# A pre-norm transformer block on one core: one key projection of 512 columns per group, and the combine weights' transposes behind the shared expert's gate and up

## The reference

```python
x = x + attn(layernorm(x), Wq, Wk, Wv, Wo)          # 16 heads of 8, local windows of 64 keys
...
scores = einsum('bhnqd,bhnkd->bhnqk', qb, k2) * scale   # mask: j > i and j <= i + 64
p = softmax(where(mask, scores, -1e30)); out = p @ v2
...
x = x + ffn(layernorm(x))
...
topk_idx, topk_weight = gate(x)                     # 16 experts in 4 groups, 2 groups and 4 experts kept
g = einsum('nh,ehm->enm', x, w_gate); u = einsum('nh,ehm->enm', x, w_up)
y = sum over experts of combine * ((silu(g) * u) @ w_down)
shared = (silu(x @ sw_gate) * (x @ sw_up)) @ sw_down
```

## Time and profile before

| | |
|---|---|
| median of 3 runs | 814.77 us (814.01 to 815.94) |
| the profiled execution | 814.36 us, of which the span from first to last instruction is 812.6 us |
| TensorE busy | 740.3 us (91%), 5984 matmuls |
| TensorE weight loads | 611.7 us (75%) |
| GpSimd / ScalarE / VectorE busy | 618.8 us (76%) / 607.7 us (75%) / 525.1 us (65%) |
| mean granted TensorE clock | 0.977 of full speed |

### The profile page before, as it was taken

One profiled execution on the slowest core, in us unless ns is written; L12 is line 12 of the kernel. 1 busy time (PEld: TensorE's weight loads), 2 busy tenths in 40 slices (PEclk: granted clock), 3 DMA queues, 4 the chain that ended last, 5 costly groups with the idle time before them and its releaser, 6 DMA issues.

```text
span 812.6 us, 19809 instructions
## 1 busy us (share of the span) xinstructions
PE 740.3 (91%) x5984; PEld 611.7 (75%) x5984; DVE 525.1 (65%) x1735; ACT 607.7 (75%) x1816; POOL 618.8 (76%) x842
## 2 busy tenths in 40 slices
PE   2568889999999999999999999999999999998876
PEld 1446668787887878787887878787887878786755
DVE  3456686767767676767667676767767575764332
ACT  4787788788787888878788788878787888863332
POOL 3525467879888888978888888988888887956876
PEclk9698899999999999999999999999999999999999
DMA  5000022040413213040312213040313203041321
GB/s 155 26 1 15 14 74 73 15 136 10 120 40 97 63 53 105 2 133 22 105 52 92 65 42 115 2 129 26 105 52 90 67 31 114 3 122 37 117 92 41
DMA packets 50738, 53.86 MB, mean 66 GB/s; under 512 B 5632, under 2 KB 31744, under 8 KB 50560
## 3 DMA queue, kind: packets, MB, share of 16 engines
q1 hardware_dynamic: 50688, 53.25, 21.5%
HBM read 44.31 MB, written 4.72 MB: 60 GB/s over the span
## 4 chain that ended last, share of the span: by engine, by line
PE 45%; POOL 26%; issue 16%; ACT 8%; DMA 2%; DVE 2%; POOLq 1%; SPq 0%; ACTq 0%; DVEq 0%
POOL gate L470 9%; PE PS L1053 8%; PE PS L979 7%; PE PS L869 7%; PE PS L911 6%; PE PS L870 5%; PE PS L871 5%; ACT probs L602 4%; POOL hh L473 4%; POOL q_lo L452 4%; POOL k_lo L462 2%; PE PS L972 2%; PE PS L1050 2%; POOL X L432 1%; PE PS L1014 1%
## 5 line engine op out<-in xcount | busy, mean ns | idle before, releaser
L602 ACT ACTIVATE probs<-PS,neg_max 128x96 f32<-128x96 f32 (+1 forms) x1024 | 245.8, 353 | 60.1 <-DVE neg_max L798 59.4
L470 POOL TENSOR_TENSOR gate<-gate,spread 128x512 f32<-128x512 f32 x128 | 164.2, 1283 | 64.4 <-DMA spread<-weights_by_expert 47.2
L750 DVE STREAM_TRANSPOSE probsT<-probs 128x384 f32<-128x384 f32 (+1 forms) x256 | 124.0, 522 | 101.8 <-ACT probs L602 101.8
L473 POOL TENSOR_TENSOR hh<-gate,tu 128x512 f32<-128x512 f32 x128 | 164.5, 1285 | 17.2 <-POOL gate L470 11.9
L786 DVE SCALAR_TENSOR_TENSOR tu<-th,PS 128x512 f32<-128x512 f32 x128 | 87.9, 687 | 89.3 <-PE PS L871 56.4
L1053 PE MATMUL PS<-wd,hh 128*128 128x128 f32 x1024 | 136.1, 276 | 9.6 <-POOL hh L473 9.6
L1053 PEld LDWEIGHTS PS<-wd,hh 128*128 128x128 f32 x1024 | 126.6, 192 | 15.1 <-POOL hh L473 9.4
L798 DVE TENSOR_REDUCE neg_max<-PS 128x4 f32<-128x384 f32 (+1 forms) x256 | 125.4, 513 | 8.2 <-PE PS L979 5.4
L869 PE MATMUL PS<-x_hi,w_hi 128*128 128x512 f32 x288 | 125.0, 434 | 1.0 <-DVE hs L834 1.0
L560 ACT ACTIVATE th<-PS 128x512 f32<-128x512 f32 x128 | 79.7, 623 | 59.6 <-PE PS L871 59.2
L871 PE MATMUL PS<-x_lo,w_hi 128*128 128x512 f32 x288 | 114.5, 397 | 0.0
(11 more groups left out here) (108 smaller groups left out, 1362.1 us busy)
## 6 DMA issues: line engine op xcount, KB each, us to landing
spread<-weights_by_expert SPq DMA_DIRECT2D x256, 128.0 KB, 3.0
X<-x SPq DMA_DIRECT2D x32, 256.0 KB, 3.4
OUT<-H SPq DMA_DIRECT2D x16, 256.0 KB, 3.0
out<-OUT SPq DMA_DIRECT2D x16, 256.0 KB, 3.1
probsT<-w_gu SPq DMA_DIRECT2D x1, 1152.0 KB, 8.0
wd<-w_down SPq DMA_DIRECT2D x1, 512.0 KB, 9.0
weights_by_expert<-cT SPq DMA_DIRECT2D x16, 32.0 KB, 1.6
probsT<-w_att SPq DMA_DIRECT2D x1, 264.0 KB, 3.5
```

Of the source, the lines that this page charges most:

```text
L470: tt(gate2[:, :], gate[:, k % 2, :], spread[:, k % SP_BUFS, :], ALU.mult).then_inc(s_g2, 1)
L473: tt(hh[:, k % 2, :], gate2[:, :], tu[:, k % 2, :], ALU.mult).then_inc(s_h, 1)
L602: ins = nc.scalar.activation(probs[:, u % 2, tt, a, j0:KW], PS[:, tt, a * KW + j0:a * KW + KW], ACT.Exp, bias=neg_max[:, tt, a:a + 1])
L750: ins = v_.transpose(probsT[:, b, :, t0 + tt, c0:3, :].rearrange("p g c q -> p g (c q)"), probs[:, u % 2, tt, :, c0 * Q:KW])
```

## The change

Two edits. First, the keys of both sequences are projected together: one use `KP = 6` in place of `(6, 8)`, so three matmuls of 512 columns in step 6 and none in step 0. `kr_hi` and `kr_lo` become 512 wide, and the later copies read their half. The shared banks get 14 uses per slot, before 15. Second, in step 3 TensorE runs `gate_up` of the shared expert before the transposes of `comb`, and ScalarE takes its tanh before it copies `cT`. VectorE's order in step 3 stays as it was.

```diff
-KP = (6, 8)
+KP = 6
...
-    (EARLY, (VP, KP[0], LG)), (LATE, (XT, QP, KP[1], XT2, XT2 + 4)),
+    (EARLY, (VP, KP, LG)), (LATE, (XT, QP, XT2, XT2 + 4)),
...
-        kr_hi = sb("kr_hi", [P, T], F32R)
-        kr_lo = sb("kr_lo", [P, T], F32R)
+        kr_hi = sb("kr_hi", [P, TOK], F32R)
+        kr_lo = sb("kr_lo", [P, TOK], F32R)
...
-                                tt(k_lo[:, a, T * b:T * b + T], kr_lo[:, :].bitcast(F32),
+                                tt(k_lo[:, a, T * b:T * b + T], kr_lo[:, T * b:T * b + T].bitcast(F32),
...
-                    def keys(b):
-                        g, _ = at(sl, s, KP[b])
-                        if g:
-                            side, bank = filled(act, sl, s, KEY_PLACE[b])
-                            if not (g.fixed and g.n == 0 and b == 0):
-                                act.wait_ge(s_k_hi, g.n * GB + b)
-                            copy(kr_hi[:, :], bank[:, 0:T]).then_inc(s_high[side], 1)
-
-                    keys(0)
+                    g, _ = at(sl, s, KP)
+                    if g:
+                        side, bank = filled(act, sl, s, EARLY)
+                        if not (g.fixed and g.n == 0):
+                            act.wait_ge(s_k_hi, g.n * GB)
+                        copy(kr_hi[:, :], bank).then_inc(s_high[side], 1)
...
+                    g, _ = at(sl, s, SH)
+                    if g:
+                        act.wait_ge(s_g, g.n * NF + 1)
+                        if not (g.fixed and g.n == 0):
+                            act.wait_ge(s_fa, g.n)
+                        nc.scalar.activation(th[:, :], PS[:, 4, :], ACT.Tanh, scale=0.5).then_inc(s_th, 1)
                     g, _ = at(sl, s, CT)
                     if g:
                         side, bank = filled(act, sl, s, WEIGHTS)
...
-                    keys(1)
...
-                    def keys(b):
-                        g, _ = at(sl, s, KP[b])
-                        if g:
-                            side, bank = free(KEY_PLACE[b])
-                            r = slice(T * b, T * b + T)
-                            exact3(bank[:, 0:T], *w2(WK), xT_hi[:, r], xT_lo[:, r]).then_inc(s_filled[side], 1)
-
-                    keys(0)
+                    g, _ = at(sl, s, KP)
+                    if g:
+                        side, bank = free(EARLY)
+                        exact3(bank, *w2(WK), xT_hi[:, :], xT_lo[:, :]).then_inc(s_filled[side], 1)
...
+                    g, _ = at(sl, s, SH)
+                    if g:
+                        gate_up(g, NP, 0)
+
                     g, _ = at(sl, s, CT)
...
-                    g, _ = at(sl, s, SH)
-                    if g:
-                        gate_up(g, NP, 0)
-
-                    keys(1)
```

More of the change, by code:

```diff
@@ L68 @@
 EARLY, POST, WEIGHTS, LATE = range(4)
-KEY_PLACE = (EARLY, LATE)
 USES = sorted([(stage % STEPS, place, stage) for place, stages in (
-    (EARLY, (VP, KP[0], LG)), (LATE, (XT, QP, KP[1], XT2, XT2 + 4)),
+    (EARLY, (VP, KP, LG)), (LATE, (XT, QP, XT2, XT2 + 4)),
     (POST, (OT, OT + 4, ON, ON + 4, OW, OW + 4)), (WEIGHTS, (CT,)))
@@ L74 @@
 assert len({use[:2] for use in USES}) == len(USES)
-SPLIT = (*zip(KEY_PLACE, KP), (LATE, XT), (LATE, QP), (LATE, XT2), (LATE, XT2 + 4))
+SPLIT = ((EARLY, KP), (LATE, XT), (LATE, QP), (LATE, XT2), (LATE, XT2 + 4))
 LOOP_FIRST, LOOP_END = 6, NG
@@ L456, in slot @@
                         if g:
-                            taken(pool, sl, KP[b] % STEPS, KEY_PLACE[b])
+                            if b == 0:
+                                taken(pool, sl, KP, EARLY)
                             if not (g.fixed and g.n == 0):
@@ L627, in slot @@
                         if g:
-                            taken(act, sl, KP[b] % STEPS, KEY_PLACE[b])
+                            if b == 0:
+                                taken(act, sl, KP, EARLY)
                             if not (g.fixed and g.n == 0):
@@ L632, in slot @@
                             for a in range(HG):
-                                ins = copy(k_hi[:, a, T * b:T * b + T], kr_hi[:, :].bitcast(F32),
+                                ins = copy(k_hi[:, a, T * b:T * b + T], kr_hi[:, T * b:T * b + T].bitcast(F32),
                                            scale=headrow[:, a:a + 1])
@@ L775, in slot @@
                                          ALU.add).then_inc(s_y, 1)
-                    keys(0)
+                    g, _ = at(sl, s, KP)
+                    if g:
+                        side, bank = high_out(sl, s, EARLY)
+                        if not (g.fixed and g.n == 0):
+                            dve.wait_ge(s_k_lo, HG * g.n * GB)
+                        split_low(kr_lo[:, :], bank, kr_hi[:, :]).then_inc(s_taken[side], 1)
                     g, _ = at(sl, s, LN1)
```

## The result

The changed kernel takes 846.47 us (median of 4 runs, 843.95 to 847.97) against 814.44 us (814.01 to 815.94): ratio 1.0387, 95% interval 1.0357 to 1.0416. It is 32 us slower, and I had forecast 8.3. The profiled execution took 843.95 us (span 841.8), 2.5 under the median.

A forecast was written before the change was run, and what follows sets the result against it. TensorE was taken as the bound, busy 44.97 of 46.0 us per slot. Terms 4.4 + 2.3 - 0.3 + 0.9 + 1.0 = 8.3 us on 814.36 gave 822.7, stated as 823, range 819 to 828.

The forecast's parts named there:

- No new wait comes of it: Shared banks, used 14 times per slot in place of 15: every fill waits as before, so no wait is added.
- Leg 1: From TensorE's XT2 transposes over ScalarE, VectorE and 18 us of GpSimd to `comb`: 23.1 us, whatever TensorE does.
- leg 2: From `comb` to the next slot's XT2 transposes, about 22.9 us on TensorE alone; added work lengthens the slot in full.
- the wait ahead of `ve`: GpSimd's idle time before L431, where leg 1 starts: to grow by about 0.5 us from 3.04 us.
- The keys: Wider projection in step 6 adds 0.34 us per slot, 4.4 us over 13; removing step 0's 0.44 us gives nothing back.
- The wait for `up_taken`: Before gate and up in step 3, ended by `tu`: 0.18 us per slot, 2.3 us in all; slot 3 gives back 0.3.
- The last slots: Later transposes and spread tiles: +0.9 us in slot 17 (between 0.4 and 1.9) and +1.0 us in slot 18.
- The clock: TensorE's granted clock in full slots stays 1.00 despite about 1.6 us idle, as after the wait at 784 to 787.
- The keys cost nothing: Rival, chance 0.12: leg 1 starts at an earlier result than TensorE's L1032, so 0.34 us is absorbed: 817.0 us.
- faster: Rival, chance 0.13: the wait for `comb` goes and `tu` comes in time, in each full slot: 801.8 us.
- no change: Rival, chance 0.07: `tu` 0.5 us earlier cancels the keys, or the tail hides its delay: 813 to 816 us.
- The clock's 841: Rival, chance 0.06: the clock falls in each slot, gate and up run at half speed, 18 us more: 841 us.

The follow-up runs named there:

- ten memsets: The changed kernel with ten 128x1 memsets more on VectorE in slot 0, ahead of its loop: 827.66 us, 1.0166 of the kernel before.
- 562: VectorE's loop start in the kernel before (814.44 us), and in the changed kernel with ten memsets in slot 0 (827.66 us).
- 692: The changed kernel with 140 memsets on VectorE ahead of its loop, which then starts at instruction 692: 827.30 us.
- 722: The changed kernel with 170 memsets on VectorE in slots 1 to 5, so that its loop starts at instruction 722: 834.04 us.
- 552: The changed kernel without padding, VectorE's loop starting at instruction 552: 846.47 us, 1.0387 of the kernel before.
- 808: The kernel before, without either edit, with 246 memsets on VectorE in slots 1 to 5, loop start 808: 831.85 us, 1.0219.
- the nine matmuls: Second edit alone, plus nine extra 128x128 matmuls on TensorE ahead of its waits for `hh` in slots 17 and 18: 822.70 us.
- the old order: Second edit alone, but slots 17 and 18 run transposes before gate and up: 818.98 us; on the whole change with ten memsets: 822.87 us.

## Why the prediction was wrong

**The step that failed** is one that isn't there: the sum counts every instruction by the engine's time for it, and none by its place in the engine's program. "No new wait comes of it" was said of semaphores, and holds for them; the new wait is for instructions. It costs 18.8 us of the 32.0 (the changed kernel with and without ten memsets), and 16 can be read off the trace: from `comb` to `comb` on GpSimd the four slots that hold a stall last 50.5 to 50.9 us, those beside them mostly 46.7.

What the runs show of it: with a body of 355 or 358 instructions, starts of 562 and 692 have no stall, 722 one of 2.6 us of idle time per turn, 552 and 808 one of 5.3 to 5.9. All five fit if VectorE holds two blocks of 256 instructions and one block ends 0 to 9 instructions behind 553, so that others end at 809 to 818 and at 1065 to 1074. At 562 and 692 the body lies within two blocks (from 692 on it ends at 1047). At 722 it ends at 1077, in a third, and the jump back finds its target gone. At 552 and 808 it spans three as well, and its first block is left within a few instructions, so that VectorE would stand still for the second block too. The Trainium skill has this rule in Runtime: NRT & Kernel Launch, section Instruction fetch mechanics: blocks of 256 instructions, two of them in most engines, and a taken branch whose target is not in the two has to wait for a fetch. The traces agree, and add the size. That it is the second block that doubles the stall at 552 is argued from the lengths 2.6 and 5.5, with as many packets at both; the blocks themselves were not seen, and their size is the page's. That the place of the loop makes the stall is shown: ten memsets take it away, and padding brings it into a kernel without either edit.

**Leg 1, leg 2** were right: the table above has +0.34 us in B for the keys, and taking away the start of leg 1 took the wait for `comb` away, with 0.8 us per slot. One sign that I had named failed: the wait ahead of `ve` was to grow by 0.5 us, and in the normal slots it is 3.12 us against 3.04.

**The keys**, 4.4: measured 5.6 with the loop in its old place. The mechanism was right; A also grows by 0.04 us (25.00 against 24.96 on the mean of two slots), 4.8 to 4.9 over 13 slots. The rest is in the tail, at which I took nothing: in the traces slot 17 is 0.8 us longer. That taking the second projection out gives nothing back is right too, but not where the time goes: 0.36 us, of which the wait for `comb` takes 0.09. And TensorE's own work falls by 0.02 to 0.03 us per slot, not 0.10.

**The wait for `up_taken`**, 2.3 - 0.3: measured 4.2. The wait stood where I put it, ended by `tu`, and the hand-over of 0.05 us held in every second slot; in the others it was 0.13. Mis-sized was what follows: the same four transposes take 0.43 us ahead of L1032 and took 0.35 ahead of gate and up, and gate and up 1.50 in place of 1.47. I had carried times from one order over to another. That is 0.28 us per slot, 0.36 in every second, and not 0.18.

**The last slots**, 0.9 + 1.0: measured 4.1 and, on the whole change, 4.8. Slot 18 is +1.0 as forecast. In slot 17 I named both ends, 0.4 and 1.9, and each came in some traces. With the second edit alone, with the nine matmuls and with ten memsets most of gate and up ran at the lower level (`cT` 1.8 to 2.0 us later behind `comb` than with the old order). In the profiled run of the changed kernel itself they ran at full speed, 1.50 us, and `cT` came 1.92 us behind the start of `comb`, before 1.49:

```profile
769.37 0.50 PE L862 MATMUL PS<-x_hi,w_hi 128*128 128x512 f32 x1 [0.99 <-DVE tu L780]
...
770.87 0.60 PE L1007 MATMUL PS<-cst,comb 128*16 128x128 f32 x4
...
780.31 1.13 PE L1041 MATMUL PS<-wd,hh 128*128 128x128 f32 x8 [3.45 <-POOL hh L473]
...
812.98 2.05 PE L1041 MATMUL PS<-wd,hh 128*128 128x128 f32 x8 [3.59 <-POOL hh L473]
```

And I had no term for what the later spread tiles do to TensorE: its wait for `hh` grows from 0.86 to 2.98 us and from 2.35 to 3.70 with the second edit alone. The eight matmuls behind it took 2.04 to 2.05 us there in place of 1.13. In the profiled run of the changed kernel they took 1.13 behind 3.45 us of wait, and 2.05 behind 3.59.

**The clock** in the full slots held, by the row at 784 to 787 that I followed: 1.00 in the normal slots with 1.28 us of idle time. In the slot with a stall that is shown above it was 0.97, in the other three 1.00.

**The rivals.** "The keys cost nothing" is out by the table, "faster" and "no change" since `tu` ends 23.2 us behind the last L1032 with the second edit as without it. The clock's 841 was near the number for another reason. Without the stall the change costs 13.5 us (827.7), at the top of the range that I gave. That is 5.2 more than the sum, in the three terms above: 5.6 + 4.2 + 4.1 = 13.9.

## What to carry to other kernels

Where a kernel has a loop on the chip, count each engine's instructions ahead of the loop and in its body before and after an edit. Here a body of 355 instructions ran free of stalls from two places and with them from two others, and removing ten instructions far ahead of it cost more than everything that the edits were priced for. The sign is idle time that ends with "issue" ahead of the body's first instruction, once in each turn. And before work is moved out from under a wait, ask which other wait it was covering: the four transposes were cover for `up_taken`, and no gain elsewhere made them dispensable.

## What the runs showed of the hardware

At the jump back of its loop VectorE stood still for 2.6 us in one kernel (start 722) and for 5.3 to 5.9 us in two (552 and 808), and not at all from 562 and 692. Of these, 1.2 and about 4 us per turn reached the slot. As for TensorE's clock, waits of nearly one length were followed by either level. Behind 2.50 us with the nine matmuls the eight down projections took 2.07 us (granted clock 0.53 from 794 to 797), behind 2.44 us with the old order in the last slots 1.73, behind 2.35 us in the kernel before 1.13, and behind 3.45 us in the changed kernel 1.13 (from 780 to 783 the granted clock there was 0.74, so it fell a little later). So the length of the wait alone doesn't tell the level, and what does is open.
